# Where a pair's six scatters stand beside the first root: four ahead of it and two behind it, in place of three and three

## What is computed

```python
h = tok(x)                                   # (64, 169, 128)
h = h + attn(layernorm(h))                   # exp features; D_inv = 1 / (q' . sum k' + 1e-6)
y = layernorm(h)
topv, topi = top_k(y @ Wg, 2); w = softmax(topv)
for e in range(8):
    hid = silu(y @ W[e]) * (y @ V[e])
    h = h + gate_w(e) * (hid @ W2[e])
```

## Time and profile before

| what | us |
|---|---|
| median of three runs | 1154.52 |
| lowest, highest | 1152.82, 1154.71 |
| the profiled execution | 1159.75 |
| its span (first to last instruction) | 1158.0 |

### The profile page before, as it was taken

How to read it: one execution, slowest core, us unless ns; L and a number is a source line. 1 busy time by engine, 2 the same in 40 slices (tenths; PEclk the granted TensorE clock), 3 DMA queues, 4 the chain that set the end, 5 groups by cost and what they waited for, 6 DMA issues and landing times.

```text
span 1158.0 us, 29957 instructions
## 1 busy us (share of the span) xinstructions
PE 1088.3 (94%) x8580; PEld 924.0 (80%) x8581; DVE 882.1 (76%) x3333; ACT 561.7 (49%) x1307; POOL 613.2 (53%) x656
## 2 busy tenths in 40 slices
PE   3899999999999999999999669999999999999995
PEld 3667777777777777777776468999999999999995
DVE  5468887888888878878867567777777777777774
ACT  3444535436355354363343424555555555555552
POOL 0103444445444454454444456586767676677675
PEclk9899999999999999999999979999999999999998
DMA  8270131301311313111010324343434343343442
GB/s 166 47 200 21 32 78 29 81 29 33 78 33 36 74 32 79 30 32 32 30 34 28 104 69 73 47 57 54 55 53 55 52 57 51 53 57 53 54 55 30
DMA packets 76011, 65.51 MB, mean 57 GB/s; under 512 B 12338, under 2 KB 66802, under 8 KB 75926
## 3 DMA queue, kind: packets, MB, share of 16 engines
q0 software_dynamic: 32704, 24.99, 15.2%
q1 hardware_dynamic: 43078, 39.16, 14.0%
q10 hardware_dynamic: 144, 0.32, 0.1%
HBM read 32.72 MB, written 31.71 MB: 56 GB/s over the span
## 4 chain that ended last, share of the span: by engine, by line
PE 79%; DVE 9%; SPq 4%; issue 3%; DMA 3%; ACT 1%; POOL 0%; POOLq 0%; DVEq 0%; ACTq 0%
PE bank L1440 21%; PE bank L1457 13%; PE bank L677 6%; PE bank L612 5%; PE bank L726 5%; PE bank L739 4%; PE bank L713 4%; PE bank L715 3%; PE bank L714 3%; PE bank L732 3%; DVE patches L824 2%; PE bank L605 2%; PE bank L476 2%; PE bank L1428 2%; DMA out_rows<-yo,dest 2%
## 5 line engine op out<-in xcount | busy, mean ns | idle before, releaser
L1612 POOL DMA_INDIRECT out_rows<-yo,dest x184 | 312.4, 1698 | 140.4 <-issue 107.0
L1440 PE MATMUL bank<-xT_e,wv 128*128 128x256 f32 x2208 | 291.9, 288 | 5.4 <-DVE xT_e L1546 3.5
L1440 PEld LDWEIGHTS bank<-xT_e,wv 128*128 128x128 f32 x2208 | 273.9, 191 | 6.1 <-DVE xT_e L1546 4.0
L1323 POOL DMA_INDIRECT sorted_rows<-xrow_all,sloti x192 | 191.4, 997 | 88.4 <-issue 52.8
L1516 ACT ACTIVATE sil<-bank 128x256 f32<-128x256 f32 x368 | 141.1, 384 | 173.0 <-PE bank L1440 152.3
L1457 PE MATMUL bank<-w,hid 128*128 x1472 | 182.0, 277 | 3.0 <-DVE hid L1553 3.0
L1457 PEld LDWEIGHTS bank<-w,hid 128*128 128x128 f32 x1472 | 173.6, 194 | 4.4 <-issue 4.4
L1553 DVE TENSOR_TENSOR hid<-sil,bank 128x256 f32<-128x256 f32 x368 | 143.9, 417 | 24.8 <-ACT sil L1516 20.9
L1535 DVE TENSOR_TENSOR wv<-wv_all,wv 128x1024 fp32r<-128x1024 f32 x92 | 113.3, 1232 | 64.4 <-PE bank L1440 48.8
L1234 ACT ACTIVATE attn<-bank 128x256 f32<-128x256 f32 x128 | 49.4, 386 | 162.1 <-issue 127.1
L1498 ACT CAST wv<-wv_all 128x1024 fp32r x92 | 96.1, 1046 | 29.4 <-issue 27.9
(11 more groups left out here) (213 smaller groups left out, 1802.8 us busy)
## 6 DMA issues: line engine op xcount, KB each, us to landing
xr<-sorted_rows SPq DMA_DIRECT2D x92, 130.0 KB
raw<-in_x SPq DMA_DIRECT2D x64, 84.5 KB
raw<-in_x SPq DMA_DIRECT2D x60, 78.0 KB
out_rows<-attn SPq DMA_DIRECT2D x64, 58.5 KB
sorted_rows<-xrow_all,sloti POOLq DMA_INDIRECT x192
out_rows<-yo,dest POOLq DMA_INDIRECT x184
wv_all<-in_L_ffn_W SPq DMA_DIRECT2D x8, 256.0 KB, 6.0
wv_all<-in_L_ffn_V SPq DMA_DIRECT2D x8, 256.0 KB, 6.2
```

Of the source, the lines that this page charges most:

```text
L1323: po.indirect_dma_start(sorted_rows, bass.IndirectOffsetOnAxis(sloti[:, p, j, ch:ch + 1], 0), xrow[:, p, j, ch], None).then_inc(s(f"scatte ...
L1440: q = pe.matmul(bank[fc][:, TT * m:TT * m + TT], wv[:, w, w_, m, cols], xT[:, p, x_], start=(w_ + x_ == 0), stop=(w_ == 1))
L1612: po.indirect_dma_start(out, bass.IndirectOffsetOnAxis(dest[:, p, a:a + 1], 0), yo[:, p, a], None, compute_op=ALU.add).then_inc(s(f"added{ ...
```

## The change

Two scatters for each of chunks 0 and 1 (four instructions) stand ahead of the first root; the two of chunk 2 stand behind it. Before, it was three and three. In the steps without a, the wait between the two parts asks for four landed scatters (64) in place of three (48).

```diff
                 if 3 < n < NPAIR + 2:
                     wait_alone(po, setup_met, (s("sloti_ready"), md), (s("w1_ready"), md), (s("d8_done"), md + 2))
-                    scatter(range(1), 1 - pd)
-                    scatter(range(1, 2), 1 - pd, (0,))
+                    scatter(range(2), 1 - pd)
                 if a:
                     wait_alone(po, setup_met, (s("ln1_mv"), NCH * (n + 1)), (s("ln1_x"), n))
                     root(rstd[:, 0], mv[:, 0, :, 1], vare[:, 0], 1e-5, K("mhalf")[:, 0:NCH], s("ln1_vare"), s("ln1_rstd"), n)
                 if 3 < n < NPAIR + 2:
                     if not a:
-                        po.wait_ge(s(f"scattered{1 - pd}"), 96 * ((md - 1) // 2) + 48)
-                    scatter(range(1, 2), 1 - pd, (1,))
+                        po.wait_ge(s(f"scattered{1 - pd}"), 96 * ((md - 1) // 2) + 64)
                     scatter(range(2, NCH), 1 - pd)
```

## The result

Of 22 runs each, taken in turns, the kernel before had a median of 1154.62 us and the changed one 1159.15 us (1152.87 to 1163.59). The ratio is 1.0031, with a 95% interval of 1.0019 to 1.0043: slower by about 3.6 us, more than the 0.2% that can be told from no change. The forecast was 1154.6. The profiled execution of the changed kernel has a span of 1161.8 us, before it was 1158.0.

What follows compares the result with a forecast made beforehand. PE bounds the kernel, busy 94% of the span with 79% of the chain. The root is 0.10 to 0.20 us late in 20 steps, of which 0.1 us reaches PE: 1154.52 to 1154.6 us, range 1152.6 to 1157.6.

Steps and rivals of the forecast that it cites:

- The room on POOL: POOL's idle 1.17 us ahead of the first root takes the fourth scatter; with a 0.01 us gap the root is 0.10 late.
- What of it reaches PE: PE's full queue at the transposes L719 hides the late xtok; only step 4 pays, 0.10 us.
- The size of that reserve: PE's slack at the transposes L719: 0.10 us in k=2 (k=0 alike), 0.34 in k=3, none in k=1.
- k=1 has no reserve and isn't late: In k=1 PE has no slack, but POOL's hole is 1.33 us, so the root isn't late at all.
- L983 has its cover: DVE's L983 comes up to 0.10 us later in ten steps, hidden by PE's own work; 1.0 us if that were gone.
- Contention: The fourth scatter beside DVE's statistics and normalise slows nothing: 0, at most 1.1 us.
- the scatters behind the root: Two instead of three on POOL end 1.26 us sooner; nobody waits for that.
- steps 32 and 33: Awaiting the fourth scatter's landing instead of the third's leaves the fifth starting when it did before: 0.
- B: Slower: POOL's root starts 0.30 us behind the fourth scatter's end instead of 0.01; 5.9 us, 1160.4; chance 0.14.
- C: Slower: POOL's descriptor queue fills with four in a row, the fourth scatter takes longer; some 5.4 us, 1160; chance 0.04.
- D: Faster: DVE gains where the sixth scatter no longer runs beside the choice of experts; 2.4 us, 1152.1; chance 0.05.

Runs made afterwards that it cites:

- with five: Five scatters ahead of the first root and one behind, in all steps with a root, against three and three before: 1200.77 us, before 1158.24 on that chip.
- late42: The changed kernel with PE's L677 waiting for DVE's fourth normalise only ahead of its fourth matmul: ratio 1.0071 to the kernel before.
- late33: The kernel before, three and three, with PE's L677 waiting for DVE's fourth normalise only ahead of its fourth matmul: ratio 0.9996.
- drain: The kernel before with four and two, and the wait for four landings, in steps 32 and 33 alone: ratio 0.9987 to the kernel before.

## Why the prediction was wrong

Forecast was 1154.6, from 1152.6 to 1157.6, with nothing to be seen; 1159.15 and 0.31% came. By its own steps:

- **The room on POOL.** Right in kind: the hole of 1.17 us is the room, k=1 has 1.33 and is not late. The gap behind a scatter was mis-sized. It was taken from the copy of the earlier trace rows, 0.01 us; ahead of the root it measured 0.07 in 25 of 27 steps, with four and with five. 0.30 + 0.96 + 0.07 = 1.33 is just the hole of k=1 and 0.16 over that of the others. The late root is 0.16 us, not 0.10. The Trainium skill (Perfetto Trace Analysis, GPSIMD Engine Instruction) warns against a GpSimd span as a measure and asks for the spacing from start to start. The trace agrees: behind a scatter with a span of 0.96 us the next scatter starts 1.26 us after its start, the root 1.03 to 1.04, the copy 0.97. One row for one kind of instruction didn't give the gap of another.
- **What of it reaches PE.** This is the step that failed. The prediction had a reserve on PE of 0.10 us in k=0 and 2, read on one path, from xtok to the transposes. But DVE's list holds the fourth normalise behind xtok, and PE's next group, L677, waits for that with a reserve of 0.00. Of 0.16 us all passed in k=0, k=2 and steps 28 to 30, and nothing in k=3 (the earlier trace rows had 0.34 there): by the rows of the step table 0.26 in step 4, five k=0 steps of 0.16, four k=2 steps of 0.15, three last ones of 0.16, and 0.23 in step 17, together 2.4, of which 2.29 is seen. Against the repeat of before, which has no late signals, it is 2.61. Even with the right gap, the argument by the transposes alone would have given 0.06 in each of the same steps and so under 1 us.
- **The size of that reserve.** late42 shows some 0.12 us on the transposes' path in k=2 and 0.09 in k=0, and the prediction's 0.10 is near them by luck. Its 0.41 us, "the least", was itself L677 waiting for the normalise (0.28 without that wait, in late33), and its 0.51 in step 18 ran to a matmul's start; to L677's weight load it was 380.92 - 380.51 = 0.41. 0.41 - 0.28 gives 0.13.
- **k=1 has no reserve and isn't late.** Right for the six k=1 steps with the hole of 1.33. Step 29 is a k=1 step too and has a hole of 1.17, so by the prediction's own rule its 0.10 should have been in the sum; it took 18.57 where it had taken 18.41. And it fails in step 17, where the idle time ahead of the root is 0.35 to 0.36 us instead of 0.07 in three executions of the changed kernel. Why isn't known.
- **L983 has its cover.** Right for a delay of 0.16 us: against the repeat of before the wait at L983 fell from 10.4 to 9.6. Step 14 of before puts the cover at some 0.8 us.
- **Contention, the scatters behind the root, steps 32 and 33.** At 0, as forecast, in the profiles of the changed kernel; the last was tried by itself (drain). What the forecast had no term for is that a scatter can stand beside a signal of PE that is seen late.
- **Rivals.** B had the right place, the right kind (a gap behind the scatter greater than 0.01) and the wrong size (0.30). Its point of decision, 0.14 us of gap for 2.3 us of time, was built on the reserve that wasn't there: without that reserve 0.07 is enough. B's 1160.4 was near the median by luck. C falls: the fourth scatter took 0.95 to 0.97 us in steps 4 to 30 and 1.02 in step 31, not over 1.1. D falls too: the steps of k=1 and k=3 are as long as before (19.44 and 19.51), none shorter.
- **The rest.** The steps' 2.3 to 2.9 us are 0.20 to 0.25%. The repeats on chips 3 and 4 give 1.0012 to 1.0025 for the change and its parts (3.1 and 2.9 us for the change at the same clock), and the interval of the first comparison begins at 1.0019. Whether the rest of its 1.0031 is late signals (forms of the change cost 1.005 to 1.007 where those are) is argued, not measured, since its chips aren't known, nor the clocks of the 22 runs of the kernel before.

## What to carry to other kernels

When an engine's result comes later, follow every instruction behind it on the engine that takes it up, not only the one that uses it: the next one in the list is late as well, and whoever waits for that has a reserve of its own. A reserve of 0.10 us is worth a look at the very next wait on the same engine, in the same rows. When two runs differ by a few tenths of a per cent, compare them at the same granted clock. And before two profiles are compared line by line, look whether they are of one kind (records lost or whole, the same waits grown everywhere); repeat both on one chip if they aren't.

## What the runs showed of the hardware

- A small POOL instruction whose waits are met starts 0.07 us behind the end of an indirect DMA's issue, a copy 0.00 to 0.01 us behind (in the changed kernel's step 32 too, below), and a second indirect DMA 0.30 us behind.

```profile
659.13 0.96 POOL L1323 DMA_INDIRECT sorted_rows<-xrow_all,sloti  x1 [0.30 <-issue]
660.10 0.51 POOL L1342 COPY xrow_all<-xrow_all 128x384 f32<-128x384 f32 x1
```

- PE's completions can be seen by ACT and DVE about 1 us late (1.10, 0.92 and 1.01 us above; L677's by 0.38 to 1.01 in twelve steps of the kernel before) in the steps in which POOL issues indirect DMAs. The same program on another chip has 0.05 to 0.10. Such executions also lose two fifths to three fifths of the trace's records of landings.
- The time from the last convolution to the first expert goes with the granted clock in it: 60.08 us at 0.90 and 62.39 at 0.86 for one and the same program, 62.09 at 0.85, 60.74 at 0.88; with ten more products 60.14 at 0.93 and 62.09 at 0.89. PE's busy time grows by nearly as much as the drain does (42.70 and 44.96, 49.09 and 51.04 us).
